# Seven block products for q, k and v, with attention in a stage of its own, on one Trainium2 core

## What is computed

```python
c = x @ W1.T + b1 + 2 * lora(x)                 # an adapter per sequence, rank 16
q, k, v = c @ wq, c @ wk, c @ wv                # 32 query heads, 8 key/value heads of 128
q, k = rope(q), rope(k)
scores = where(allowed, q @ k.T * 128**-0.5, min)      # causal, window 256: here just causal
x1 = x + softmax(scores) @ v @ wo               # 4 query heads share a key/value head
h = x1 @ W2.T + 2 * lora_of_two_experts(x1)     # routed by token
out = x1 + h @ Wf.T + bf + 0.5 * lora_of_two_experts(h)
```

## Time and profile before

| | us |
|---|---|
| median of three runs | 2875.87 |
| lowest, highest | 2873.94, 2877.47 |
| the profiled execution | 2878.1 |
| its span, first to last instruction | 2876.3 |
| mean granted TensorE clock | 0.996 |
| HBM read and written, MB | 151.55, 22.22 |

### The profile page before, as it was taken

How to read it: one execution, slowest core, us unless ns; L and a number is a source line. 1 busy time by engine, 2 the same in 40 slices (tenths; PEclk the granted TensorE clock), 3 DMA queues, 4 the chain that set the end, 5 groups by cost and what they waited for, 6 DMA issues and landing times.

```text
span 2876.3 us, 37235 instructions
## 1 busy us (share of the span) xinstructions
PE 2827.7 (98%) x13944; PEld 2321.0 (81%) x13944; DVE 1482.6 (52%) x2187; ACT 498.2 (17%) x657; POOL 485.2 (17%) x198
## 2 busy tenths in 40 slices
PE   8989999999999999999998999999999999999999
PEld 7867888888888888878877788888888888887887
DVE  2131556465655646565523255646556564656452
ACT  2122112111111211131202211112111111212110
POOL 0020212112111211210303021111112111221030
PEclk9999999999999999999999999999999999999999
DMA  6841111111111111101442111111111111110232
GB/s 209 234 137 37 45 44 36 44 43 43 37 44 44 41 46 36 44 29 60 109 136 73 44 44 37 44 44 36 44 44 44 40 40 44 37 43 29 80 94 69
DMA packets 230717, 174.57 MB, mean 61 GB/s; under 512 B 65146, under 2 KB 198394, under 8 KB 230658
## 3 DMA queue, kind: packets, MB, share of 16 engines
q1 hardware_dynamic: 202850, 151.77, 18.1%
q10 hardware_dynamic: 27808, 22.02, 2.4%
HBM read 151.55 MB, written 22.22 MB: 60 GB/s over the span
## 4 chain that ended last, share of the span: by engine, by line
PE 89%; DVE 7%; issue 3%; ACT 1%; DMA 0%; SPq 0%; DVEq 0%; ACTq 0%
PE prod L542 27%; PE prod L544 26%; PE prod L543 26%; PE turned L741 2%; DVE x L1457 2%; PE turned L719 2%; PE turned L536 1%; PE prod L638 1%; PE prod L904 1%; PE turned L729 1%; DVE row_max L1397 1%; DVE rope_sin L1384 1%; DVE row_sum L1406 1%; DVE probs L1394 1%; PE turned L709 0%
## 5 line engine op out<-in xcount | busy, mean ns | idle before, releaser
L542 PE MATMUL prod<-c_hi,w_hi 128*128 128x512 f32 (+1 forms) x1856 | 735.0, 396 | 3.2 <-DVE c_lo L1468 3.2
L544 PE MATMUL prod<-c_hi,w_lo 128*128 128x512 f32 (+1 forms) x1856 | 723.7, 390 | 0.0
L543 PE MATMUL prod<-c_lo,w_hi 128*128 128x512 f32 (+1 forms) x1856 | 722.7, 389 | 0.0
L1205 POOL TENSOR_TENSOR w_lo<-raw,w_hi 128x1024 fp32r<-128x1024 f32 x160 | 389.0, 2431 | 1785.5 <-ACT w_hi L999 1785.5
L1457 DVE TENSOR_TENSOR x<-prod,x 128x512 f32<-128x512 f32 x512 | 345.9, 689 | 268.9 <-PE prod L544 268.9
L542 PEld LDWEIGHTS prod<-c_hi,w_hi 128*128 128x128 f32 (+1 forms) x1856 | 347.4, 187 | 79.2 <-DVE c_lo L1468 4.0
L544 PEld LDWEIGHTS prod<-c_hi,w_lo 128*128 128x128 f32 (+1 forms) x1856 | 347.3, 187 | 75.6
L542 PE MATMUL prod<-o_hi,w_hi 128*128 128x512 f32 x1024 | 405.7, 396 | 0.0
L543 PEld LDWEIGHTS prod<-c_lo,w_hi 128*128 128x128 f32 (+1 forms) x1856 | 347.7, 187 | 71.4 <-issue 1.0
L544 PE MATMUL prod<-o_hi,w_lo 128*128 128x512 f32 x1024 | 399.1, 390 | 0.0
L543 PE MATMUL prod<-o_lo,w_hi 128*128 128x512 f32 x1024 | 398.8, 389 | 0.0
(11 more groups left out here) (123 smaller groups left out, 2209.9 us busy)
## 6 DMA issues: line engine op xcount, KB each, us to landing
raw<-in_wq SPq DMA_DIRECT2D x64, 512.0 KB, 4.0
raw<-in_wo SPq DMA_DIRECT2D x64, 512.0 KB, 3.7
raw<-t_scratch SPq DMA_DIRECT2D x34, 512.0 KB, 3.5
t_scratch<-x ACTq DMA_DIRECT2D x17, 512.0 KB, 4.9
x_raw<-in_x SPq DMA_DIRECT2D x16, 512.0 KB, 8.2
raw<-in_wk SPq DMA_DIRECT2D x16, 512.0 KB, 3.5
raw<-in_wv SPq DMA_DIRECT2D x16, 512.0 KB, 3.6
raw<-m_scratch SPq DMA_DIRECT2D x16, 512.0 KB, 3.5
```

The source lines that it names most:

```text
L542: pe.matmul(dst, wh, xh, start=start, stop=False)
L543: pe.matmul(dst, wh, xl, start=False, stop=False)
L544: return pe.matmul(dst, wl, xh, start=False, stop=stop)
L1205: pool.tensor_tensor(WL[j % 2][:], RAW[j % 2][:], WH[j % 2][:].bitcast(F32), ALU.subtract).then_inc(split_d, 1)
```

## The change

**q, k, v by seven products.** Two weight columns of 128 make a pair (k and v of a group, query heads 0 and 1, heads 2 and 3). The pair is a block product: 2 halves of the contraction by 2 columns for the weights, 2 halves by 2 token tiles for c. Instead of eight block products (two outputs by two tiles by two halves, 12 matmuls each) it makes seven, P1 to P7, on sums of blocks, in the order P1, P6, P2, P5, P7, P4, P3. The sums of c, `T1`, `T2`, `T4` and one more in place of a block of c, are made once per half, in the W1 stage and behind it. The sums of weights (S2 and the operands of P5, P7, P3) are made by GpSimd for each pair, and so are the seven low parts; ScalarE casts the seven high parts. P2 adds into P1's bank, P7 into P6's, P3 into P5's. VectorE forms the outputs from the banks and ScalarE's copy of P1: `U2 = P1 + P6`, C11 is P2's bank, `U3 = P1 + P7's bank`, `C22 = U3 + P5`, `C21 = U3 - P4`, `C12 = U2 + P3's bank`. C11 and C12 are the first column for both tiles, C21 and C22 the second (for kv: v).

**A stage of its own.** The 24 pairs of a half run one behind the other with attention between their products (`attention`), a unit spread over two pairs; the wo blocks of all eight groups follow as a stage. o goes to DRAM in float32 (`o_store`) and comes back for wo, where it is split again. `T1` and `T2` lie where `X1` was, so `X1` is written to DRAM in the W1 stage and read back before wo.

**Softmax.** VectorE only takes the maximum and scales it by a tiny operation; ScalarE takes it off as the bias of the exponential, which is therefore made for each of the 8 sequences of a unit, 128x64, and gives the row sums by `accum_out`.

The diff, cut to its core:

```diff
-    for j in range(12):                                     # TensorE, per group
-        main(Q_G + j, (j // TT) % 2, j % TT, CH, CL).then_inc(prod, 1)
-        ...
+P1, P6, P2, P5, P7, P4, P3 = range(7)
+BANK = {P1: 2, P6: 3, P2: 2, P5: 1, P7: 3, P4: 0, P3: 1}
+def pair(B, lp):                                            # TensorE
+    for n in range(NP):
+        attention(B, lp, n)
+        ...
+        pe.wait_ge(s_lo, B["s_lo"] + (NP * lp + n + 1 + 14))
+        if n == P2:
+            pe.wait_ge(p1_in, B["p1s"] + (lp + 1))
+        else:
+            last = {P1: C11 - NC, P6: U3 - NC, P5: C12 - NC, P4: C21 - NC, P7: U2, P3: C22}[n]
+            pe.wait_ge(comb, B["comb"] + (NC * lp + last + 6))
+        for k in range(4):
+            ...
+            mm = three(PJ[BANK[n]][:], slot_hi(n)[:, ks], slot_lo(n)[:, ks], xh, xl, ...)
+def attention(B, lp, n):                                    # lp % 3: KV, Q01, Q23
+    if lp % 3 != Q01 and lp >= 2:      # scores before P6 and P5, turn before P4, pv before P3
+        e = 4 * ((lp - 1) // 3) + 2 * (lp % 3 == KV)
+        ...
+    if lp % 3 != Q23 and lp >= 3:      # turn_p(e + 1) before P1, pv(e + 1) before P6
+        ...
+    if lp % 3 == Q01 and n in (2, 3):
+        turn_v(B, lp // 3, n - 2)
+def weights(B, lp):                                         # GpSimd, all 128x512
+    add(S2F[:], a21, a11, ALU.subtract)
+    add(S2F[:], S2F[:], a22, ALU.add)
+    lo(P1, a11)
+    lo(P6, S2F[:])
+    lo(P2, a12)
+    add(SLF[P5][:, NT:2 * NT], a21, a22, ALU.add, P5)
+    lo(P5, ...)
+    add(SLF[P7][:, NT:2 * NT], a11, a21, ALU.subtract, P7)
+    lo(P7, ...)
+    lo(P4, a22)
+    add(SLF[P3][:, NT:2 * NT], a12, S2F[:], ALU.subtract, P3)
+    lo(P3, ...)
+def pair(B, lp, last=False):                                # VectorE
+    if host is not None:
+        before_exp(B, host)
+    dve.tensor_tensor(a1, P1S[:], bank[P6], ALU.add)        # U2
+    turn(0, dst[0], view(bank[P2], SPT), SPT, 1, comb, ...) # rotary turn of C11, from PSUM
+    if host is not None:
+        before_exp(B, host + 1)
+        normalise(B, host)
+    dve.tensor_tensor(b0, P1S[:], bank[P7], ALU.add)        # U3
+    dve.tensor_tensor(b1_, b0, bank[P5], ALU.add)           # C22
+    if host is not None:
+        normalise(B, host + 1)
+    dve.tensor_tensor(b0, b0, bank[P4], ALU.subtract)       # C21
+    if kind != KV:
+        turn(1, both, view(CB[:, 2 * NT:4 * NT], TT * SPT), TT * SPT, 0, roped, ...)  # 128x1024
+    dve.tensor_tensor(a1, a1, bank[P3], ALU.add)            # C12
+    turn(1 if kind == KV else 2, dst[1], view(a1, SPT), SPT, 0, roped, ...)
+def turn(n, out, x, segs, c, signal, value):                # sines, cosine, sum
+    ...
+def exp(B, u):                                              # ScalarE
+    for b in range(SPT):
+        ins = act.activation(SM[:, c:c + SEQ], SM[:, c:c + SEQ], ACT.Exp, bias=MX[:, m:m + 1],
+                             scale=SM_SCALE, accum_out=SUM[:, m:m + 1])
-        dve.tensor_tensor(..., MX[:, ms]..., ALU.subtract)  # before_exp
-        dve.tensor_reduce(SUM[:, ms], view(SM[:, ws], SPT), AX.X, ALU.add)
+        dve.tensor_scalar(MX[:, ms], MX[:, ms], -SM_SCALE, None, ALU.mult)
+def pair(B, lp, last=False):                                # ScalarE, its order
+    take_p(B, spill); weight_hi(B, lp, P3); p1_copy(B, lp); weight_hi(B, lp + 1, P1)
+    o_store(B, spill); exp(B, host); weight_hi(B, lp + 1, P6); take_v; weight_hi(B, lp + 1, P2)
+    take_v; exp(B, host + 1); weight_hi(B, lp + 1, P5); take_p(B, host)
+    weight_hi(B, lp + 1, P7); weight_hi(B, lp + 1, P4); o_store(B, host)
+for b in range(TB):                                         # SP, behind the b rows
+    sp.wait_ge(x_res, hf * TB + (b + 1))
+    sp.dma_start(view(x1_d, KC)[:, :, b * P:(b + 1) * P], view(X1[:], KC)[:, :, b * P:(b + 1) * P])
```

More of the change, by code:

```diff
@@ new lines, in _ @@
+                names = ("comb", "tb", "qk", "unit", "s_lo", "p1s")
+                B = a_bases(pe, hf, 0, names)
+                for lp in range(2):
+                    pair(B, lp)
+                with pe.Fori(0, LOOPS) as turn:
+                    B = a_bases(pe, hf, turn, names)
+                    for lp in range(2, 8):
+                        pair(B, lp)
+                B = a_bases(pe, hf, LOOPS, names)
+                for lp in range(2, 6):
+                    pair(B, lp)
+                TAIL = {0: [(turn_p, 5)], 2: [(pv, 5)], 3: [(score, 6)], 6: [(score, 7)], 10: [(turn_p, 6)],
+                        11: [(pv, 6)], 12: [(turn_p, 7)], 14: [(pv, 7)]}
@@ L918, in _ @@
             act.sem_inc(tb_taken, 1)
+            act.sem_inc(o_copied, 1)
+            for w in range(2):
+                act.sem_inc(o_out[w], 16)
             def wf_hi(b):
@@ L992, in _ @@
                 act.copy(AH[:], AW[:]).then_inc(hi_done, 1)
[L994 to L999 removed]
                 def b1_cols(s, j):
                     act.copy(view(BC[s][:], TT), view(B1S[:], TT)[:, :, bass.ds(j, P)]).then_inc(bc_in, 1)
[L1004 removed]
+                A_NAMES = ("a_prod", "comb", "s_sum", "raw", "unit", "tb", "stored", "head")
@@ L1101, in _ @@
+                g0 = act.snap(hf * 0)
+                group(g0, 0, first=True)
+                with act.Fori(0, NKV // 2 - 1) as it:
+                    for par in (1, 0):
+                        group(act.snap(it * 2 + (2 - par)), par)
+                group(act.snap(g0 + (NKV - 1)), 1, last=True)
                 act.wait_ge(prod, q_base + (Q_3 - 8))
@@ L1457, in _ @@
                         dve.tensor_tensor(X1[:, xs], PJ[q % 4][:], X1[:, xs], ALU.add).then_inc(taken, 1)
-                        for f, u in after.get(i, ()):
-                            f(u)
+                        if first:
+                            for f, u in TAIL.get(i, ()):
+                                f(B, u)
+                            if i == 12:
+                                o_lo(0, 1, og)
+                        if not last and i == 24:
+                            o_lo(1 - par, 0, on)
+                        if not last and i == 30:
+                            o_lo(1 - par, 1, on)
+                g0 = dve.snap(hf * 0)
+                group(g0, 0, first=True)
+                with dve.Fori(0, NKV // 2 - 1) as it:
+                    for par in (1, 0):
+                        group(dve.snap(it * 2 + (2 - par)), par)
+                group(dve.snap(g0 + (NKV - 1)), 1, last=True)
                 dve.wait_ge(taken, q_base + (Q_3 + 4))
```

946 lines of the change are left out of this document (664 added, 282 removed).

## The result

The changed kernel takes 2934.91 us (median of 4 runs, 2934.39 to 2936.61), the kernel before 2875.36 beside it (4 runs). The ratio is 1.0208, with a 95% interval of 1.019 to 1.0225: slower, by 1.9 to 2.25%. The profiled execution took 2936.6 us, its span 2934.7.

The account below looks back on a forecast made before the run. The prediction took TensorE's matmul count times pace as the bound: 2878.1 - 130.6 (matmuls removed) - 15.4 (old stall) + 85 (new stalls) + 24 (edges) gave 2841, stated as 2840 us, range 2765 to 2905.

Parts of the forecast that it names:

- What is removed: q, k, v products on TensorE: 576 matmuls at 0.2267 us, 130.6 us off; also the old 15 us stall for probabilities.
- ScalarE: New stage: 128x64 exponentials at 0.33 us, 2.7 a unit; in all 33 of 72 us a group, not a bound.
- Rival 3: Exponentials with a sum cost 0.6 us or more, delaying the first normalisation and C21: 2880 us; chance 0.10.
- GpSimd: New stage: 12 operations of 128x512 a pair at 1.31 us each, 47.3 us a group.
- VectorE: New stage: 46.5 us a group; operations reading two SBUF tensors lock with GpSimd, 2.3 us at 1024 columns.
- The walk: One group of the new stage followed in order: score blocks wait for VectorE's rotations, 5.5 us a group, 85 us in all.
- 2756 + 16 s: The forecast's general formula for the run time in us, s being the stall per group.
- (a): Residual stores on SP's queue delay the next W1 block's load: TensorE waits 4.5 us each half, bounds 0 and 20.
- (b): Entry into the new stage: T4's VectorE chain is late for P4, 4 us each half, bounds 2 and 8.
- (c): Entry into wo: VectorE's backlog while X1 and o come back, 2 us each half, bounds 0 and 8.
- Rival 1: The SBUF port lock hardly matters because VectorE falls into GpSimd's holes; s near 1, 2772 us; chance 0.28.
- Rival 2: The port pair shared by GpSimd and VectorE is itself the bound; s = 10, 2916 us; chance 0.20.

Follow-up runs that it names:

- e3_late_scores: Changed kernel with both score blocks of a pair one product later and, on VectorE, the first normalisation before the second mask; 2894.41 us, ratio 1.0059.
- e5_order: e3_late_scores with turned probabilities copied before the second unit's exponentials on ScalarE, and the second unit normalised after the fourth combination on VectorE; 2834.55 us, ratio 0.9851.
- e1_short_turn: Changed kernel with the second head's rotary turn made for only 1 of 16 sequences from the third pair of a half on; 2807.25 us.
- e2_early_p1: Changed kernel with ScalarE copying P1 before the casts of P5, P7, P4, P3 and T4 at the stage's start; 2935.16 us, ratio 1.0193.
- e4_filler: Changed kernel with 12 or 6 useless matmuls added on TensorE ahead of the first score block of a pair; 2881.11 us, ratio 1.0008.
- e6_edge: e5_order with P1 copied earlier in the first two pairs and T4 made in sixteen operations of 512 columns, not four of 2048; 2831.61 us, ratio 0.9847.
- e7_old_softmax: Changed kernel with the softmax of before: VectorE subtracts maxima and sums rows, ScalarE makes one 128x512 exponential; 2945.38 us, ratio 1.0237.
- e8_light_pool: Changed kernel with 5 of 12 GpSimd operations a pair, and two ScalarE casts, cut to 8 of 512 columns from the second pair on; 2819.53 us.
- e9_before_pause: Kernel before, with the last addition of the third rotation done nine times in place of once on VectorE; 2981.59 us, ratio 1.0364.
- e10_before_short: Kernel before, with the last addition of the third rotation done six times in place of once on VectorE; 2916.6 us, ratio 1.0136.

## Why the prediction failed

I had 2840 us and a range to 2905; it was 2935, and slower than before where I gave faster 0.73. In the order of its steps:

- **What is removed.** 576 matmuls are gone from the count, and their pace is still 0.2267 us where the clock is full. Of the old stall of 15 us 1.9 stayed.
- **ScalarE.** Taken 0.33 us apiece, 2.7 a unit. The groups by line have 335 ns and 187 ns for an exponential and the reading of its sum, which overlap: starts are 0.33 us apart (600.86 and 601.21, then 601.55, in e3_late_scores). Rival 3 is out.
- **GpSimd.** Taken 1.31 us; 1.29 alone, on average 1.29 to 1.96 by group of operations with VectorE beside it, so 56.9 us busy a group where I had 47.3.
- **VectorE.** Taken 2.3 us for a locked operation of 1024; 2.16 and 2.12, and 1.73 for the sines on 64 partitions (above). The four together take 8.04 us here, 590.49 to 598.53, where the walk had 8.1. Its timeline at the pause:

```profile
589.68 0.69 DVE L1940 TENSOR_TENSOR combined<-combined,prod 128x512 f32<-128x512 f32 x1 [1.15 <-PE prod L715]
590.49 3.60 DVE L1901 TENSOR_TENSOR rope_sin<-combined,consts_sb 64x1024 f32<-64x1024 f32 x2
594.10 2.22 DVE L1903 TENSOR_TENSOR q_rot<-combined,consts_sb 128x1024 f32<-128x1024 f32 x1
596.36 2.17 DVE L1905 TENSOR_TENSOR q_rot<-q_rot,rope_sin 128x1024 f32<-128x1024 f32 x1
```

- **The walk**, which I called the term that decides. Stalls of 3.4 and 2.1 us, 5.5 a group; measured 3.7 and 1.7, 5.4 a group, 80.9 in all against 85. It was right, and so was the cause that it named.
- **What failed: the price of a stall.** The sum set each microsecond of pause at one microsecond, and gave the clock a part of the 12 us of a half's edges alone; the groups had nothing for it, and no reason was given. The 30 pauses of the groups, 1.7 to 3.7 us each, were followed by 25 stretches at the lower clock, 21 of 6.8 us and 4 of 3.4: one behind each of the 16 pauses of 2.8 to 3.7 us, and one behind 9 of the 14 of 1.7. In a group with two of the long ones that is 6.8 us on top of 5.4. In "2756 + 16 s" s was (2936.6 - 2756) / 16 = 11.3, not 5.5. The clock term is 82.2 us above that of before, and all waits 106.1, where my terms make -15.4 + 85 + 24 = 93.6: 2841.1 + 82.2 + 12.5 = 2935.8. The trace of before had no pause over 1.0 us within the groups, and its clock of 1.00 was taken as a property of the chip instead of one of a TensorE that hardly waits. At its edges the same trace had the sign: a wait of 5.6 us, up to 164.7, with 6.8 us at the lower level from 163.7, and one of 3.5 with 13.7.
- **The edges.** (a) 4.5 us; it was 2.1 in one half. (b) 4 us with 2 to 8 as bounds; it was 14.4 in the first half, with 13.7 us at the lower clock, of which 10 lie inside the pause and cost nothing. The step counted T4's chain on VectorE alone and not what it meets there: GpSimd's sums, and behind them ScalarE's casts and the copy of P1. (c) 2 us; there is no wait of this kind at the start of wo.
- **Rivals.** Rival 1 is out: the lock held 30 of the 32 operations of L1903. Rival 2 gave 2916 through the port as the bound, s = 10. The number was nearer than my forecast, by luck, as the mechanism wasn't this: in no group did TensorE wait for GpSimd's halves, and with the order changed (e5_order) the same operations fit into 76.5 us.

The Trainium skill has the failed step: "TensorE: Matmul & The Clock Gate", HAM oscillation — how this bites in real kernels, tells of a kernel whose bursts each start slow again because a wait lies between them, and takes half of the slowed time as the cost. The runs here agree in the price: half of 6.8 us a pause. The waits told of there are 3 to 5 us long; here 1.7 us brought the lower clock in 9 of 14 cases, and 1.4 us in 8 of 16.

The sum for all runs, us (the waits as the profile counts them, with their number, then with 0.16 us more for each):

| profiled execution | waits | their term | clock term | sum | measured |
|---|---|---|---|---|---|
| changed kernel | 146.4 (63) | 156.5 | 90.5 | 2935.8 | 2936.6 |
| e1_short_turn | 91.5 (50) | 99.5 | 19.0 | 2807.3 | 2807.3 |
| e2_early_p1 | 145.4 (69) | 156.5 | 100.3 | 2945.6 | 2943.4 |
| e3_late_scores | 143.5 (90) | 157.9 | 52.6 | 2899.3 | 2898.0 |
| e4_filler (62.6 more) | 94.5 (78) | 107.0 | 10.4 | 2868.8 | 2876.1 |
| e5_order | 106.2 (87) | 120.1 | 17.4 | 2826.3 | 2834.9 |
| e6_edge | 103.0 (92) | 117.7 | 18.2 | 2824.7 | 2831.1 |
| e7_old_softmax | 152.4 (63) | 162.5 | 93.9 | 2945.2 | 2945.4 |
| e8_light_pool | 90.8 (48) | 98.5 | 29.9 | 2817.2 | 2819.5 |
| e9_before_pause (130.6 more) | 103.9 (52) | 112.3 | 54.7 | 2986.4 | 2982.7 |
| e10_before_short (130.6 more) | 70.3 (53) | 78.8 | 21.5 | 2919.7 | 2917.4 |

Eight of the eleven come out within 4 us, the three others 6 to 9 us short.

## What to carry to other kernels

Where TensorE is the bound at full clock, price a new pause of two to four microseconds at its length and some three microseconds of clock, and look at the granted clock beside the waits; two pauses a group can turn a gain of 130 us into a loss of 60. Pauses of up to one microsecond cost little more than their length here, so spread the waits by the order on each engine before taking work out. When a wait is moved, walk the lists of all engines again: ScalarE's order gave the next wait twice here.

## What the runs showed of the hardware

- The granted clock falls behind short pauses: 3.6 us in every group of the old kernel cost 57.7 us of waiting and 46.4 us of clock; 1.4 us brought the lower level in half of the groups; the pauses of up to 1.0 us in e5_order twice, behind 2 of the 28 ahead of a score block.
- Useless matmuls can pay: 62.6 us of them made the kernel 54 us faster.
- Cutting an operation doesn't shorten a shared wait: T4's 2048 columns took 3.2 us whole and 5.6 us in four pieces beside GpSimd, while GpSimd's sums went from 3.3 to 1.74.
- The tiny scaling of the row maximum (8 elements a partition) takes 0.17 us alone and 1.07 in this row of e3_late_scores, where a sum of GpSimd ran from 607.19 to 608.48:

```profile
607.44 1.07 DVE L1865 TENSOR_SCALAR row_max<-row_max 128x8 f32<-128x8 f32 x1
```

The prediction had left that out, as a rule of the Trainium skill without a row here ("SBUF — State Buffer", Who interferes with whom). The row bears the rule out, but over the changed kernel it is small: the mean of the line is 0.24 us there (0.64 in e3_late_scores).
